# Transposing the slot logits later and in two pieces, in a fused vision-transformer step

## The reference, cut to what matters

```
logits = einsum('sd,btd->bst', sl, tok)            # 64 slots x 196 tokens of an image
dispatch_w = softmax(logits, axis=-1)              # over the tokens
combine_w = softmax(logits, axis=-2)               # over the slots
y = einsum('btd,bst->bsd', xn, dispatch_w)         # the slot inputs
...
out = einsum('bsd,bst->btd', y, combine_w)
```

```
energy = einsum('bhnd,bhmd->bhnm', q, k) * decay
out = einsum('bhnm,bhmd->bhnd', energy, v)
```

## Time and profile before

| | us |
|---|---|
| median of 3 runs | 1220.85 |
| lowest and highest | 1219.61 and 1221.07 |
| the profiled execution | 1220.71 |
| its span in the trace | 1219.0 |

### The profile page before, as it was taken

One profiled execution on the slowest core, in us unless ns is written; L12 is line 12 of the kernel. 1 busy time (PEld: TensorE's weight loads), 2 busy tenths in 40 slices (PEclk: granted clock), 3 DMA queues, 4 the chain that ended last, 5 costly groups with the idle time before them and its releaser, 6 DMA issues.

```text
span 1219.0 us, 35974 instructions
## 1 busy us (share of the span) xinstructions
PE 1105.5 (91%) x13418; PEld 889.2 (73%) x13418; DVE 787.8 (65%) x2082; ACT 750.0 (62%) x1745; POOL 595.9 (49%) x942
## 2 busy tenths in 40 slices
PE   4899999999999999999999999999998999997563
PEld 3787888888888888888888888788886556564332
DVE  5577766677777777676777777777774222222996
ACT  5567677777777776777777777776763111110676
POOL 3366655565555666555655555665533000000664
PEclk9999999999999999999999999999999999998555
DMA  4411121111111111211111111112063999995786
GB/s 151 197 51 55 58 84 59 62 53 53 53 53 53 53 53 55 80 66 61 55 53 53 53 53 53 53 53 77 32 263 129 368 424 423 424 423 181 235 264 183
DMA packets 50718, 158.41 MB, mean 130 GB/s; under 512 B 5386, under 2 KB 31392, under 8 KB 38372
## 3 DMA queue, kind: packets, MB, share of 16 engines
q1 hardware_dynamic: 33080, 145.09, 32.2%
q10 hardware_dynamic: 17600, 12.78, 3.4%
HBM read 132.23 MB, written 25.62 MB: 129 GB/s over the span
## 4 chain that ended last, share of the span: by engine, by line
PE 71%; DVE 22%; issue 2%; ACT 1%; DVEq 1%; SPq 1%; DMA 1%; POOL 0%; ACTq 0%; POOLq 0%
DVE p_sb L828 9%; PE ps L974 8%; PE ps L976 7%; PE ps L975 7%; PE ps L1271 6%; PE ps L1052 5%; PE ps L1089 4%; PE ps L1290 4%; PE ps L1134 4%; DVE gn L803 3%; PE ps L1031 3%; PE ps L1032 3%; PE ps L1019 2%; PE ps L1157 2%; DVE res L943 2%
## 5 line engine op out<-in xcount | busy, mean ns | idle before, releaser
L427 POOL TENSOR_TENSOR xl<-x_sb,xh 128x392 fp32r<-128x392 f32 x192 | 189.8, 1026 | 84.1 <-DVE gn L803 74.9
L828 DVE TENSOR_TENSOR p_sb<-ps,dec 98x1568 f32<-98x1568 f32 x96 | 171.6, 1788 | 14.8 <-PE ps L1052 14.8
L678 ACT ACTIVATE hg<-ps 128x768 f32<-128x768 f32 x32 | 25.9, 810 | 146.0 <-PE ps L1295 146.0
L768 DVE BATCH_NORM_STATS2 st<-ps 98x6 f32<-98x192 f32 x128 | 40.0, 354 | 77.5 <-PE ps L1019 77.5
L935 DVE COPY y2st<-ps 128x192 f32<-128x192 f32 x32 | 11.4, 358 | 120.5 <-PE ps L1271 120.5
L695 ACT ACTIVATE o_sb<-res,nb,rstd 98x192 f32<-98x192 f32 x128 | 59.5, 535 | 44.8 <-DVE nb L958 44.1
L1089 PE MATMUL ps<-p_sb,vpad 98*32 98x98 f32 x3072 | 84.9, 250 | 1.6 <-DVE p_sb L828 1.6
L1319 PE MATMUL ps<-y2b,cbuf 64*98 64x192 f32 x256 | 49.3, 537 | 38.1 <-POOL y2b L532 38.1
L1089 PEld LDWEIGHTS ps<-p_sb,vpad 98*32 98x32 f32 x3072 | 64.1, 109 | 26.7 <-issue 26.2
L519 POOL CAST pickb<-pick 128x128 fp32r (+1 forms) x32 | 9.4, 293 | 148.8 <-PE ps L1295 148.8
L974 PE MATMUL ps<-xl,wh 128*128 128x392 f32 x192 | 70.1, 365 | 13.1 <-POOL xl L427 13.1
(11 more groups left out here) (203 smaller groups left out, 3484.8 us busy)
## 6 DMA issues: line engine op xcount, KB each, us to landing
x_sb<-in_xT SPq DMA_DIRECT2D x32, 1176.0 KB, 5.2
w1v<-in_fc SPq DMA_DIRECT2D x32, 1152.0 KB, 10.2
w2v<-in_fc SPq DMA_DIRECT2D x32, 1152.0 KB, 12.7
h_dram<-h SPq DMA_DIRECT2D x32, 294.0 KB
h2r<-h_dram SPq DMA_DIRECT2D x32, 294.0 KB
out<-o_sb ACTq DMA_DIRECT2D x32, 294.0 KB
comb_dram<-cst SPq DMA_DIRECT2D x32, 98.0 KB, 1.7
cbuf<-comb_dram SPq DMA_DIRECT2D x32, 98.0 KB, 3.8
```

The source lines that it names most:

```text
L427: pool.tensor_tensor(xl[:, k], x_sb[:, k], xh[:, k].bitcast(F32), ALU.subtract)\
L828: dve.tensor_tensor(dst, src, rate.unsqueeze(2).to_broadcast([T, 4, 2, TOK]), ALU.mult)\
```

## The change

The four tile products of `logits_turned` become two transposes of 98x128, each of the two images' tiles side by side. For that the four tiles lie in `Lt` (and so in `Lc`, `Ec`, `Cn`) in the order tile, image instead of image, tile; POOL's `combine_weights`, which rearranged them so far, copies them straight. In PE's list `logits_turned` goes behind `states`, `carried` 0 ahead of `dispatch_turned`, and `values` 2 ahead of `slot_inputs`; the waits of `carried_ready` go ahead of `values` 1. In DVE's list `slot_maxima` goes behind `decay` 1. The diff, whole:

```
--- before.py
+++ after.py
@@ -502,10 +502,8 @@
 
             def combine_weights(j):
                 pool.wait_ge(crec_rdy, j + 1)
-                pool.tensor_tensor(Cn[:, :, :].rearrange("p (k a) s -> p a k s", a=2),
-                                   Ec[:, :, :].rearrange("p (a k) s -> p a k s", a=2),
-                                   crec[:, :].rearrange("p (a k) -> p a k", a=2).unsqueeze(3)
-                                   .to_broadcast([T, 2, 2, S]), ALU.mult).then_inc(Cn_rdy, 1)
+                pool.tensor_tensor(Cn[:, :, :], Ec[:, :, :], crec[:, :].unsqueeze(2).to_broadcast([T, 4, S]),
+                                   ALU.mult).then_inc(Cn_rdy, 1)
             phase1(pool, step)
 
 
@@ -839,7 +837,7 @@
                 dve.wait_ge(lg_mm, j + 1)
                 dve.wait_ge(cosc_rdy, j + 1)
                 lg = ps[0:T, 6:8, LG_AT:LG_AT + 2 * S].rearrange("p x (t s) -> p x t s", s=S)
-                dve.tensor_tensor(Lt[:, :, :].rearrange("p (x t) s -> p x t s", x=2), lg,
+                dve.tensor_tensor(Lt[:, :, :].rearrange("p (t x) s -> p x t s", x=2), lg,
                                   cosc[:, :].rearrange("p (x t) -> p x t", x=2).unsqueeze(3)
                                   .to_broadcast([T, 2, 2, S]), ALU.mult).then_inc(Lt_rdy, 1)
                 dve.wait_ge(Lt_rdy, j + 1)
@@ -906,9 +904,9 @@
                                       ps[0:T, 6, 0:2 * D].rearrange("p (h d) -> p h d", d=HD),
                                       kdec[:, :].unsqueeze(2).to_broadcast([T, 2 * H, HD]),
                                       ALU.mult).then_inc(kts_rdy, 1)
+                    decay(i, 1)
                     if d:
                         slot_maxima(i - 2)
-                    decay(i, 1)
                     dve.wait_ge(s_mm, i + 1)
                     dve.tensor_tensor(state[:, :, :].rearrange("p x (q d) -> p x q d", d=HD),
                                       ps[:, 7, 0:6 * HD].rearrange("p (x q d) -> p x q d", q=2, d=HD),
@@ -1138,9 +1136,7 @@
             def logits_turned(j):
                 pe.wait_ge(Lt_rdy, j + 1)
                 for k in range(2):
-                    for a in range(2):
-                        mm = pe.matmul(ps[64 * a:64 * a + 64, 0, k * T:(k + 1) * T],
-                                       Lt[0:T, 2 * a + k, :], ident[0:T, 0:T], start=True, stop=True)
+                    mm = pe.transpose(ps[:, 0, k * T:(k + 1) * T], Lt[0:T, 2 * k:2 * k + 2, :], ident[0:T, 0:T])
                 mm.then_inc(lt_mm, 1)
 
             def dispatch_turned(j):
@@ -1222,32 +1218,32 @@
                         pe.wait_ge(Lt_rdy, i - 1)
                     rows_of_v(i, 1)
                     keys_turned(i)
+                    scores(i, 1, c)
+                    values(i, 0)
+                    states(i)
                     if d:
                         pe.wait_ge(g_sb, 2 * i + 1)
                         logits_turned(i - 2)
-                    scores(i, 1, c)
-                    values(i, 0)
-                    states(i)
                     scores(i, 2, c)
-                    if not d:
-                        carried_ready(i)
+                    carried_ready(i)
                     values(i, 1)
                 if d:
+                    if not a:
+                        idle_products(1, 16 if c else 4)
                     if a:
-                        carried_ready(i)
-                    else:
-                        idle_products(1, 16 if c else 4)
+                        carried(i, 0)
                     dispatch_turned(i - 2)
                     if not a:
                         idle_products(1, 2)
                 if a:
-                    carried(i, 0)
+                    if not d:
+                        carried(i, 0)
+                    values(i, 2)
                 if d:
                     if a:
                         pe.wait_ge(g_sb, 2 * i + 2)
                     slot_inputs(i - 2)
                 if a:
-                    values(i, 2)
                     carried(i, 1)
                 if d:
                     if c and not a:
```

## The result

The changed kernel takes 1252.97 us (median of 4 runs, 1251.79 to 1253.63) and the kernel before 1220.96 us (4 runs): ratio 1.0262, 95% interval 1.0245 to 1.028. It is slower by 32.0 us; the forecast was 1253.7. The profiled execution took 1251.79 us with a span of 1249.3. Two of the kernels further down each had one execution far longer than the rest (3451.37 and 1722.16 us), which is left out of their times.

The account below looks back on a forecast made before the run. It took PE's work and waits (71% of the chain) as the bound: 30 steps x 1.11 us = 33.3, less 0.3 for steps 32 and 33, on 1220.71 gives 1253.7 us. Bounds 1246 to 1262; stated range 1241 to 1262.

Parts of the forecast that it names:

- Es late: Slot softmax on ACT: with the maxima behind decay 1, Es starts 0.67 us late and decay 2 starts at 514.32.
- PE idle ahead of values 2: PE meets values 2 before decay 2 ends, its cover having moved behind it, and idles about 1 us.
- 0.3 us taken off for steps 32 and 33: Turned logits in the last two steps: nothing covers them there, so the new form's 0.17 us saving shows, 0.3 in all.
- release at values 2: PE starts values 2 0.15 us behind decay 2's end, as in step 0, which is 0.14 us later than now.
- wait for ysb: End of PE's step: PE waits for ysb within 0.57 us that carried 1 and Cn's turn (0.30, 0.23) fit into.
- The form and the layout: Turned logits and Lt: two transposes save 0.17 us of PE ahead of a wait; layout's DVE write unchanged; both taken as 0.
- The new place of the turned logits: Behind the states, in PE's 1.02 us before scores 2: cost 0; without that cover 0.39 us a step, 11.7 us.
- The trade of carried 0 and dispatch: On PE ahead of values 2: they only trade places, PE is through both at 515.22 as now, so no cost.
- The gain that I bounded at 0.08 us a step: Place ahead of scores 1 that the turned logits leave: at most 0.08 us a step, 2.4 us in all; taken as 0.
- Rival A: Slot inputs' new place costs, late maxima don't, Es starting at 512.24 anyway: 0.44 us a step, 13 us, 1234; chance 0.06.
- Rival B: Not slower: PE's step end has slack because something else releases the next embedding; 1218 to 1221 us; chance 0.06.
- Rival C: PE's new 1 us wait lets the granted clock fall each step: 60 to 180 us more, 1310 and above; chance 0.04.

Follow-up runs that it names:

- undo runs: Changed kernel with turned logits and slot maxima back in their old places, 1233.9 us; changed kernel with PE's old end and late maxima kept, 1221.85 us.
- token run on the kernel before: Kernel before with the fourth DVE token tile moved from ahead of decay 0 to behind kts: 1217.35 us, ratio 0.9975.
- old end: Changed kernel with PE's step end as before (dispatch, carried 0, slot inputs, values 2, carried 1), late slot maxima kept: 1221.85 us, ratio 1.0011.
- carried 0 first: Kernel before with carried 0 ahead of the turned dispatch and its waits ahead of values 1: 1235.31 us, ratio 1.0119.
- five passes: Changed kernel with the slot maxima done five times, four of them into spare columns: 1334.84 us, ratio 1.0934.

## Why the prediction was right

**The sum.** Steps longer by 1.05 us were measured and 1.11 forecast. Es late by 0.66 (0.67 forecast), decay 2 with it, PE idle ahead of values 2 (0.94 us, "about 1"), the slot inputs behind them, ysb and its turn behind those: each step is in the table above within 0.10 us. The undo runs show that it is these two parts and their meeting: each alone gives 0.04 and 0.40 us a step, both 1.05. The 0.3 us taken off for steps 32 and 33 are not seen: phase 2 starts 31.7 us later where 30 steps make 31.5, and the run with the transposes alone gained nothing. That the time came within 0.7 us of the forecast is in part luck, for 30 steps that are 0.06 us shorter than forecast make 1.8 us.

**Mis-sized.** The release at values 2, one of the two terms that I called weak: I took 0.15 us from step 0, and it was 0.05 (532.24 to 532.29), as at scores 2; why step 0 took 0.15 is not shown. Of the 0.10 us some came back behind it: the next embedding starts 0.32 us behind the second part of ysb's turn (534.82 to 535.14), where it was 0.27 before. The period ends 0.06 us under the forecast. The wait for ysb came as forecast: between 100 and 900 us the profile names `ysb` as the releaser of its turn in 12 of 27 steps, 1.8 us in all, 0.15 us each.

**Costs taken as nothing.** The form and the layout: shown by the run with the transposes alone. The new place of the turned logits: they lie inside PE's wait for decay 1. The trade of carried 0 and dispatch: right here, but only because values 2 stand between (the copy `DT` ends at 531.78, 1.33 us ahead of the slot inputs); I argued it from PE's end alone and didn't name ACT's copy, which without that cover costs 14.3 us.

**The gain that I bounded at 0.08 us a step** is 0.14 by the token run on the kernel before: I counted it from the modelled end of the turned logits. It did not enter the sum, since without an earlier decay 0 nothing of it shows: with the logits moved and the old end, scores 1 start 4.40 us behind `Lt` (506.12 to 510.52), before 4.41.

**Rival A** did not come, since Es waits for `lneg`, but it has the size given to it: its condition, a decay 2 that is not late in this order, was made in two ways and gave 1233.9 and 1233.65 for the 1234 worked out. **Rival B** is out: the next step took nothing back. **Rival C**, given 0.04, did not come, but I had argued too little against it: the wait ahead of values 2 is 0.94 us without a fall, and with 0.27 us more it fell, twice in one execution.
The Trainium skill (TensorE: Matmul & The Clock Gate, Part 4: PE-mode transpose) would have had the two transposes speak for C; in the steps 2 to 31 of the changed kernel and of the run with transposes only nothing of it is seen, and both stand at 1.00 there. The latter falls once, in step 32 (921 to 925); so does the kernel with carried 0 first (935 to 939), which has the old products, so that the transposes need not be the cause.

## What to carry to other kernels

Before work is moved ahead of other work on an engine, ask what the other work was covering: here slot inputs of 0.87 us hid the lateness of a product on another engine, and moving them behind it and making that product later cost 13.0 and 0.9 us apart, 32 together. A wait that is emptied is no gain by itself; it is room, and pays only when the thing waited for is made earlier (one token tile moved on DVE: 8 us with that room, 3.7 without). A further delay in a step of a dense PE loop can cost more than its length, since the clock can fall behind it.

## What the runs showed of the hardware

The granted clock didn't fall gradually with PE's wait. Per step, ahead of values 2, in one profiled execution each: 0.94 us, no fall in 30 steps; 1.21 us, two places; 1.36 us, 25 places (one of them in step 32) and 126 us at 0.50, which is 1.2 of the 2.4 GHz. With five passes the same 1.36 us and a further 0.59 ahead of values 1 gave no more: 18 places, 126 us. Two further passes of a 0.27 us maximum thus cost 75 us over the changed kernel where 16 are their own. Filling the wait of 1.36 us with products that nobody uses took 58 us away again, so that idle PE was the cause is shown; where exactly it begins is not.

One wait of the same length can be followed by a fall or not. In step 32 each of the fourteen kernels has PE wait for `Lt`, 1.98 to 2.00 us in thirteen of them and 1.72 in one. In five profiled executions the clock then stood at 0.50 for 3.4 us, in the other nine, the kernel before and the changed one among them, it stayed at 1.00. What decides it stays open.
